# Attention of sixteen heads: scores of a whole batch in four 32-row tiles per visit, in place of two visits of two 64-row tiles

## The reference

```python
def layer(x, context):                      # layers 1 and 2; 32 batches, 128 tokens, 256 features
    x = norm1(x + attention(q=x, kv=x,       mask=mask1))
    x = norm2(x + attention(q=x, kv=context, mask=mask2))   # layer 2: no mask here
    return norm3(x + relu(x @ w1 + b1) @ w2 + b2)           # hidden width 1024

def attention(q, kv, mask):
    Q, K, V = q @ wq + bq, kv @ wk + bk, kv @ wv + bv       # split in 16 heads of 16 features
    p = softmax(Q @ K.T / sqrt(16) + masked)                # per head 128 x 128
    return (p @ V) @ wo + bo
```

## Time and profile before

| | us |
|---|---|
| median of 3 runs | 3744.31 (3732.96 to 3747.83) |
| the profiled execution | 3738.52 |
| its span | 3736.8 |
| busy: PE, DVE, ACT, POOL | 3314.4, 2052.0, 1931.9, 1686.7 |

### The profile page before, as it was taken

How to read it: one execution, slowest core, us unless ns; L and a number is a source line. 1 busy time by engine, 2 the same in 40 slices (tenths; PEclk the granted TensorE clock), 3 DMA queues, 4 the chain that set the end, 5 groups by cost and what they waited for, 6 DMA issues and landing times. The chain is left out here.

```text
span 3736.8 us, 77616 instructions
## 1 busy us (share of the span) xinstructions
PE 3314.4 (89%) x26224; PEld 2677.5 (72%) x26224; DVE 2052.0 (55%) x4094; ACT 1931.9 (52%) x7894; POOL 1686.7 (45%) x2020
## 2 busy tenths in 40 slices
PE   8999996889999997499999999748999999976887
PEld 5988894688888887267777777626777777754664
DVE  3455553444444443356666666535666666744665
ACT  2444442333434333266666666426666666634775
POOL 1223221034344445235666666623565665662444
PEclk9999998999999999699999999969999999997999
DMA  3111113110111110311111111021111111102331
GB/s 112 48 46 65 62 34 119 52 36 19 45 48 48 48 45 32 108 55 47 58 49 58 60 53 52 21 101 47 48 52 56 41 54 56 41 29 94 98 97 54
DMA packets 192550, 213.56 MB, mean 57 GB/s; under 512 B 30208, under 2 KB 161536, under 8 KB 189696
## 3 DMA queue, kind: packets, MB, share of 16 engines
q1 hardware_dynamic: 192384, 211.40, 17.6%
HBM read 131.59 MB, written 58.72 MB: 51 GB/s over the span
## 5 line engine op out<-in xcount | busy, mean ns | idle before, releaser
L1514 ACT ACTIVATE third_stage<-third_psum,third_neg_max 128x128 f32<-128x128 f32 x1024 | 363.2, 387 | 27.1 <-DVE third_neg_max L1490 26.6
L1514 ACT ACTIVATE second_stage<-second_psum,second_neg_max 128x128 f32<-128x128 f32 x1024 | 363.2, 387 | 23.4 <-DVE second_neg_max L1490 21.9
L1496 DVE COPY second_stage<-second_psum 128x512 f32<-128x512 f32 x256 | 175.6, 686 | 134.4 <-PE second_psum L1449 133.6
L1496 DVE COPY third_stage<-third_psum 128x512 f32<-128x512 f32 x256 | 175.6, 686 | 122.9 <-PE third_psum L1449 122.2
L1514 ACT ACTIVATION_READ_ACCUMULATOR second_stage<-second_psum,second_neg_max 128x1 f32 x1024 | 232.3, 227 | 0.0
L1514 ACT ACTIVATION_READ_ACCUMULATOR third_stage<-third_psum,third_neg_max 128x1 f32 x1024 | 232.3, 227 | 0.0
L1490 DVE TENSOR_REDUCE second_neg_max<-second_psum 128x4 f32<-128x512 f32 x256 | 175.0, 684 | 102.2 <-PE second_psum L1438 102.0
L1490 DVE TENSOR_REDUCE third_neg_max<-third_psum 128x4 f32<-128x512 f32 x256 | 174.9, 684 | 85.3 <-PE third_psum L1438 85.3
L534 POOL TENSOR_TENSOR cross_ff_hidden_lo<-cross_ff_relu,cross_ff_hidden_hi 128x256 fp32r<-128x256 f32 x128 | 93.3, 730 | 283.4 <-DVE cross_ff_hidden_hi L529 283.4
L1514 ACT ACTIVATE fourth_stage<-fourth_psum,fourth_neg_max 128x128 f32<-128x128 f32 x512 | 182.2, 387 | 3.5 <-DVE fourth_neg_max L1490 3.5
L1449 PE MATMUL third_psum<-third_eye,third_stage 128*128 128x128 f32 x1024 | 156.6, 276 | 6.2 <-DVE third_stage L1496 5.8
(11 more groups left out here) (432 smaller groups left out, 12443.4 us busy)
## 6 DMA issues: line engine op xcount, KB each, us to landing
second_stage<-second_a_k SPq DMA_DIRECT2D x512, 16.0 KB, 1.8
third_stage<-third_a_k SPq DMA_DIRECT2D x512, 16.0 KB, 1.8
cross_arena<-in_l0b_packed SPq DMA_DIRECT2D x6, 1024.0 KB, 4.9
self_arena<-in_l0a_packed SPq DMA_DIRECT2D x4, 1024.0 KB, 6.2
self_x_raw<-in_x_t SPq DMA_DIRECT2D x8, 512.0 KB, 3.8
self_x_rows<-in_x_rows SPq DMA_DIRECT2D x8, 512.0 KB, 3.8
self_ct_raw<-in_ctx_t SPq DMA_DIRECT2D x8, 512.0 KB, 4.4
context_hi<-self_ct_hi SPq DMA_DIRECT2D x8, 512.0 KB, 5.0
```

The lines of the kernel that those rows point to most:

```text
L1496: dve.tensor_copy(self.sh.p_turned[:, h % 4, :, :], psum[:, TURN_BANK, :].rearrange("p (x k) -> p x k", x=4)) \
L1514: ins = act.activation(self.sh.p[:, h % 4, x, :], psum[:, SCORE_BANKS[h % 4], x * SEQ:(x + 1) * SEQ], ACT.Exp, bias=self.sh.neg_max[:, h % ...
```

## The change

In `phase16_full` the class `Attend16` is replaced by `AttendWide`; the last layer keeps `Attend16`.

- Scores are made once for a batch, for all sixteen heads: four row tiles of 32 rows (two heads each) by 256 columns, for c = 0 and then c = 1, into the two halves of the four score banks. That is 8 matmuls of 32 rows and 256 columns in place of 4 of 64 rows and 512 columns; the mask matmuls stay four for a batch, now all in front. The visit claims all four banks, and its first one in a round waits for both halves of the key blocks.
- The mix is made once for a batch (16 matmuls, then the two transposes).
- The probabilities have eight slots in place of four; the key blocks are half as wide.
- The streams of all five engines are written anew in four steps for each round (x0, x1, y0, y1), one for each batch of each attention. A step has three batches: `after` (scores, maxima, exponentials), `here` (transposes), `before` (mix, normalisation). On TensorE a step begins with the scores of `after`, the first transposes of `here` and then the mix of `before`. The drain behind the last round is one round longer (`END`).

```diff
+class AttendWide(Attend16):
+    visits = B2
+    def pe_scores(self, pe, r, banks, b):
+        if b == 0:
+            pe.wait_ge(self.proj.q_ready.sem, self.proj.q_ready.at(r, 1))
+            for c in range(C):
+                pe.wait_ge(self.proj.k_blocked[c].sem, self.proj.k_blocked[c].at(r, 16 * 8))
...
+        banks.claim(pe, r, *SCORE_BANKS)
...
+            for bank in SCORE_BANKS:
+                pe.matmul(banks.psum[:, bank, :].rearrange("p (x k) -> p x k", x=4),
+                          self.mask.value_eye[:], flags.unsqueeze(1).broadcast_to([P, 4, SEQ]),
+                          start=True, stop=False)
+        for c in range(C):
+            for t, bank in enumerate(SCORE_BANKS):
+                rows = slice(32 * t, 32 * t + 32)
+                ins = pe.matmul(banks.psum[:, bank, c * T2:(c + 1) * T2].rearrange("p (e k) -> p e k", e=2),
+                                self.proj.q[rows, c, tokens], self.proj.k_block[rows, c, :, tokens],
+                                start=self.mask is None, stop=self.mask is None or c == C - 1)
+        ins.then_inc(self.scores_ready.sem, 1)
+        for t, bank in enumerate(SCORE_BANKS):
+            banks.read(bank, self.exp_done, 4 * b + t + 1, r=r)
...
+            def start(before, here, after):        # TensorE
+                if after:
+                    att, n, b = after
+                    att.pe_scores(pe, n, banks, b)
+                turn(here, 0)
+                if before:
+                    att, n, b = before
+                    att.pe_mix(pe, n, banks, b)
...
+                start(*y1)
+                if ok(-2):
+                    ff.pe_out(pe, Back(r, 2), banks, 0, norm3.sum_ready)
+                if ok(0):
+                    pe.wait_ge(layer.ct_loaded.sem, layer.ct_loaded.at(r, 32))
+                    proj2.pe_k(pe, r, banks, ct)
+                turn(y1[1], 1)
+                if ok(-2):
+                    ff.pe_out(pe, Back(r, 2), banks, 1, norm3.sum_ready)
+                    ff.pe_hidden(pe, Back(r, 2), banks, 2)
+                turn(y1[1], 2)
+                if ok(0):
+                    norm1.pe(pe, r, banks)
+                turn(y1[1], 3)
+                if ok(-3):
+                    norm3.pe(pe, Back(r, 3), banks)
...
+                exp(y1_next, 0)                    # ScalarE
+                spread(y1)
+                if ok(0):
+                    proj2.act_k(act, r, psum)
+                exp(y1_next, 1)
+                if ok(-2):
+                    ff.act_relu(act, Back(r, 2), psum, 2)
+                hi(y1)
+                exp(y1_next, 2)
+                if ok(0):
+                    norm1.act(act, r, psum)
+                exp(y1_next, 3)
```

More of the change, by code:

```diff
@@ L2015, in _ @@
                 body(r)
-            for r in range(LAST - 1, END + 1):
+            for r in range(LAST - 1, END):
                 body(r)
@@ L2023, in _ @@
             layer.act_setup(act)
[L2025 to L2061, removed]
-                        norm3.act(act, Back(r, 3), psum)
@@ L2152, in body, with norm, first_half @@
+            def norm(before):
+                if before:
+                    att, n, b = before
+                    att.dve_norm(dve, n, psum, b)
+            def first_half(before, here, after):
+                maximum(after, 0)
+                maximum(after, 1)
+                mixed(before)
+                turned(here, 0)
+                maximum(after, 2)
+                norm(before)
+                maximum(after, 3)
+                turned(here, 1)
             def body(r):
                 ok = exists(r)
-                steps(r, ok, True)
@@ L2174, in make_flags, with inverse, lo @@
                     m.pool(pool, r, att.scores_ready)
+            def inverse(here):
+                if here:
+                    att, n, b = here
+                    att.pool_inverse(pool, n, b)
+            def lo(before):
+                if before:
+                    att, n, b = before
+                    att.pool_lo(pool, n, b)
             def body(r):
                 ok = exists(r)
-                first, second = Back(r, 1), Back(r, 2)
+                x0, x1, y0, y1 = steps(r, ok)
+                inverse(x0[1])
+                if ok(0):
+                    layer.pool_residual(pool, r, norm1.sum_ready)
+                if ok(-3):
+                    norm2.pool_rows(pool, Back(r, 3), (norm3.sum_ready, 0))
+                lo(x0[0])
+                if ok(-3):
+                    ff.pool_lo(pool, Back(r, 3), 4)
@@ L2214, in body @@
                 if ok(0):
                     make_flags(mask[1], att2, r)
+                    norm1.pool_hat(pool, r)
+                inverse(y1[1])
+                lo(y1[0])
                 if ok(-2):
-                    norm2.pool_rows(pool, second, (norm3.sum_ready, 0))
-            for m, att in zip(mask, (att1, att2)):
-                if m is not None and m.per_batch and att is att1:
-                    m.pool(pool, 0)
+                    ff.pool_lo(pool, Back(r, 2), 2)
+            if mask[0] is not None and mask[0].per_batch:
+                mask[0].pool(pool, 0)
```

417 lines of the change are left out of this document (262 added, 155 removed).

## The result

The changed kernel takes 3881.61 us (median of 4 runs, 3874.83 to 3886.3) against 3741.19 for the kernel before on the same chip: ratio 1.0375, interval 1.0348 to 1.0403. It is slower, as forecast, but by 140 us where 47 were forecast, and 12 us beyond the range.

The account below looks back on a forecast made before the run. PE bound the kernel before; after the change, a ring of scores, maximum, exponentials on ScalarE would. `second` +27 and `third` +20 us on 3738.5 gave 3785.5, plus 5.8 for the median: 3791 us, range 3715 to 3870.

Parts of the forecast that it names:

- The scores: On PE, a batch's 16 passes of 256 columns run four row tiles wide and take 1.07 us.
- PE's own work: Scores, mix and fewer changes between transposes and products save PE 5.3 us a round.
- The waits for ScalarE: PE idles before masks (2.1 us behind x1, 0.95 behind y1) and 1.7 us before norm3's transposes.
- The ends: First scores wait for 16 DMAs, +5 us a phase; the longer drain adds 10.6 in `second`, 10.8 in `third`.
- granted clock 1.00: Sign that the forecast is right: clock stays 1.00 while PE is busy 86 to 90% in `second`.
- the table: Five engine queues of a round laid out from measured distances; its 1.8% was put at 30 us either way.
- 7.2 us of waits: PE's waits in a round: those for exponentials, 1.7 for norm3, and four of 0.6 for the shared bank.
- 51.4: Forecast length in us of a steady round of `third`, against 50.9 before.
- scores of 0.92: Lower bound for a batch's scores at the mix's 0.9 ns a column; total some 25 us less.
- PE stays the bound: Rival: the new waits don't come; 3605 us, or 3704 with half the waits gone; chance 0.14 in part or whole.
- no change: Rival: savings and waits balance, waits 1.5 us a round less than worked out; 3748 us; chance 0.16.
- Row tiles aren't four wide: Rival: a batch's scores take 2.14 us, 3928 us; with only loads one behind another, 3879; chance 0.10.

Follow-up runs that it names:

- e1: The changed kernel plus 20 matmuls a round whose result nobody reads, at x1's end and around norm3's transposes; 3844.83 us.
- e7: The changed kernel with each score bank claimed singly, x1's and y1's hi and x1's relu set later, six unread matmuls ahead of norm3's transposes; 3751.47 us.
- e9: The changed kernel with each score bank claimed singly, more ScalarE jobs behind exponentials, one y0 product moved, four unread matmuls ahead of norm3's transposes; 3721.37 us.
- e5: The changed kernel with seven unread matmuls ahead of norm3's transposes and four behind them, none at x1's end; 3849.03 us.

## Why the prediction was wrong

Right, by its own steps:

- **The scores**: 1.07 us forecast, 1.07 measured; masks with a change of tiling 0.97 for 0.95; no bound by the weight loads. Four records of L1574 run at once (slice of 2006.70 to 2006.72 us).
- **PE's own work**: 5.3 us a round saved forecast, 5.0 measured. e1 shows it at full clock: idle for 30 of 500 us in `third`, 3.2 a round of 52.9, and 20 fills of 0.25 us (nine took 2.26): 52.9 - 3.2 - 5.0 = 44.7 us of work, where the earlier trace rows give 490/500 x 50.7 = 49.7.
- **The waits for ScalarE**: where, by whom, and how long: in `second` 2.01 for 2.1, 1.60 for 1.7, 0.67 for 0.95 us; ScalarE's own for the maximum 15 us a round for 13.
- **The ends**: 144.6 - 55.7 - 50.6 = 38 us for 31.

**The step that failed** is the one that made the waits' lengths into a time: "Right: granted clock 1.00", and a wait priced at its own length. The kernel before has a clock of 1.00 with PE busy for 99%; the forecast made PE idle 2 us at a time and kept the clock. e1 measures that term: 27.1 + 18.1 = 45 us. Added to the forecast it gives 3836, inside the range; the range's upper end had been drawn from the row tiles and the table's error, and the clock was in neither.

**The other half**, 48 us (19.3 in `second`, 29.0 in `third`), is the table's own error. The forecast put it at 30 us from the last layer, where the table was 1.8% short; here it was 3.2%. In a steady round of `second` e1 is 0.7 us above the table (53.8 against 53.1). In `third` the changed kernel's rounds without a fall can be taken apart. PE idles 15.04 of 105.67 us, 7.5 a round, and works for 45.3. The forecast's 7.2 us of waits are those of `second`; for `third` its 51.4 leaves 5.8 of new ones (51.4 - 50.9 + 5.3), some 6.8 with the 1.0 that PE idled before. Four terms make up the 1.4 us:

- 0.7 for waits, 7.5 against 6.8. The forecast's list lacks the 0.8 for VectorE's copy; it looked at VectorE's order in one place only, ahead of the third maximum, and found no cost. In y0 of `third` VectorE splits norm2's result first (L1730 and L1732, 3.2 us from 2968.85), then takes two maxima, and begins the copy at 2973.21; PE has had the transposes for it done since 2969.6 and the next ones, which want the bank that it empties, start at 2974.02.
- 0.3 for work saved that was counted too high (5.0 for 5.3).
- 0.6 for work between the waits that is longer than in e1 (45.3 against 44.7).
- 0.2 the other way, since the table's round before was 50.9 and the measured one 50.7.

A row suggests where the 0.6 are: x1's third transposes take 0.35 us to the next start when a product follows (2014.19 to 2014.54), and the last ones, from 2015.77, their whole recorded 0.60 before the wait that ends at 2018.38:

```profile
2014.19 0.60 PE L1585 MATMUL second_psum<-second_eye,second_stage 128*128 128x128 f32 x4
2014.54 0.37 PE L97 MATMUL second_psum<-second_w_hi,second_ff_hidden_lo 128*128 128x256 f32 x1
```

0.25 us for each of the three waits that e1 lacks would be 0.75. That is argued from rows; no run isolates it. The rest of the 48 us lies in the first rounds of the phases (above), where the clock also has a part; how it divides there stays open.

One sum of the prediction does not come out: scores of 0.92 in place of 1.07 us would save 0.15 x 128 = 19 us, not some 25. Nothing rests on it.

The rivals: *PE stays the bound* and *no change* fell with the first view. *Row tiles aren't four wide* would have given 3879 or 3928, close to the measured time, and is wrong: the scores' own row reads 1.07. A time that fits a rival is no evidence for it.

## What to carry to other kernels

A clock of 1.00 that was measured with TensorE busy for 99% is not safe in a kernel where it waits: when a change makes it wait for about 2 us at a time, price the wait and then the work behind it at the lower clock, and look for later waits that take the lateness up. Before widening a visit, draw the ring from a bank's claim through its last reader back to the claim, and put nothing into it that can stand behind: here a claim for each bank and three jobs moved on a two-thirds idle engine decided between +140 and +23 us, and a few more between +23 and -17.

## What the runs showed of the hardware that was not expected

- Idle stretches of 2.01 us can halve TensorE's clock for some 3 us and more (above). The same kernel's stretch at 2045 us, 1.60 us idle, 0.65 of transposes and 0.67 idle, was not followed by a fall, others like it were.
- Filling such a wait with matmuls that nobody reads is worth more than it costs where falls were left: 37 us with 20 a round (e1), 7 to 13 us with 6 (e7). Where hardly any were left, four a round (e9) changed nothing clear of noise.
- A fall of the clock can cost nothing: in e5's `third` rounds with one are 52.9 us and rounds without 53.0, since two later waits of 0.81 and 0.62 us are gone.
- Sixteen passes of 32 rows by 256 columns in fp32 on four row tiles take 1.07 us at full clock and 2.02 us with the clock at 0.50.
